# Spreading the reciprocal row sums of attention by two DMAs instead of by TensorE and ScalarE

## What is computed

```python
q, k, v = x @ Wq + bq, x @ Wk + bk, x @ Wv + bv      # (2048, 512), 8 heads of width 64
scores  = einsum('bdsh,bdth->bdst', q, k) / sqrt(8)
weights = softmax(scores, axis=-1)                    # over the 2048 keys
feats   = einsum('bdst,bdth->bdsh', weights, v)
out     = feats @ Wo + bo
x       = layernorm(x + out)
```

## Time and profile before

| | us |
|---|---|
| median of 3 runs | 1293.24 (1292.84 to 1294.88) |
| span of the profiled execution, first to last instruction | 1289.5 |
| the profiled execution's own time | not among the times shown; the median stands 3.7 above the span |
| attention, first spreading to last | 161 to 936 |
| PE busy (share of span) | 1255.7 (97%) |
| DVE busy | 998.2 (77%) |
| ACT busy | 919.8 (71%) |
| POOL busy | 513.2 (40%) |

### The profile page before, as it was taken

One profiled execution on the slowest core, in us unless ns is written; L12 is line 12 of the kernel. 1 busy time (PEld: TensorE's weight loads), 2 busy tenths in 40 slices (PEclk: granted clock), 3 DMA queues, 4 the chain that ended last, 5 costly groups with the idle time before them and its releaser, 6 DMA issues. The chain is left out here.

```text
span 1289.5 us, 24161 instructions
## 1 busy us (share of the span) xinstructions
PE 1255.7 (97%) x8128; PEld 1058.8 (82%) x8128; DVE 998.2 (77%) x1891; ACT 919.8 (71%) x1643; POOL 513.2 (40%) x508
## 2 busy tenths in 40 slices
PE   7999999999999999999999999999988999999896
PEld 5888799889889889989989989989866877777642
DVE  5623688789889979979979979979866777776387
ACT  5421589778878868868868868878833877778343
POOL 0002223234524524524533533542543666676412
PEclk9999999999999999999999999999999999999999
DMA  8788466212424424323423423543578999997698
GB/s 282 258 283 289 155 196 223 69 42 84 147 66 138 145 70 139 125 88 110 146 84 101 155 89 88 156 136 120 178 272 326 386 386 385 346 339 252 237 426 335
DMA packets 90951, 253.14 MB, mean 196 GB/s; under 512 B 16824, under 2 KB 39480, under 8 KB 87504
## 3 DMA queue, kind: packets, MB, share of 16 engines
q1 hardware_dynamic: 70608, 196.78, 44.9%
q0 software_dynamic: 17920, 50.62, 10.2%
q10 hardware_dynamic: 2304, 4.20, 0.8%
HBM read 177.87 MB, written 134.91 MB: 243 GB/s over the span
## 5 line engine op out<-in xcount | busy, mean ns | idle before, releaser
L967 ACT ACTIVATE p_hi<-slot 128x512 fp32r<-128x512 f32 x512 | 278.5, 596 | 108.9 <-PE slot L1594 105.5
L807 POOL TENSOR_TENSOR p_lo<-prob,p_hi 128x512 fp32r<-128x512 f32 x128 | 166.1, 1297 | 441.9 <-ACT prob L969 441.7
L1607 PE MATMUL slot<-k_stack,q_stack 128*128 128x512 f32 x1024 | 300.1, 415 | 0.0
L984 ACT ACTIVATE prob<-prob,row_min 128x1024 f32<-128x1024 f32 x256 | 296.8, 1160 | 0.1
L1307 DVE TENSOR_TENSOR p_lo<-slot,p_hi 128x512 fp32r<-128x512 f32 x384 | 250.8, 681 | 52.5 <-ACT p_hi L967 51.1
L1594 PE MATMUL slot<-ident,prob 128*128 128x128 f32 x2048 | 265.8, 273 | 1.3 <-ACT prob L984 1.3
L1632 PE MATMUL pv_acc<-p_hi,v_pair 128*128 128x256 f32 x1024 | 263.1, 290 | 2.6 <-POOL p_lo L807 1.8
L1632 PE MATMUL pv_acc<-p_lo,v_pair 128*128 128x256 f32 x1024 | 253.7, 281 | 0.0
L1594 PEld LDWEIGHTS slot<-ident,prob 128*128 128x128 f32 x2048 | 229.5, 141 | 1.9 <-issue 1.7
L1632 PEld LDWEIGHTS pv_acc<-p_hi,v_pair 128*128 128x128 f32 x1024 | 192.6, 188 | 16.1 <-issue 5.7
L1632 PEld LDWEIGHTS pv_acc<-p_lo,v_pair 128*128 128x128 f32 x1024 | 192.8, 188 | 12.9 <-issue 3.3
(11 more groups left out here) (196 smaller groups left out, 1974.4 us busy)
## 6 DMA issues: line engine op xcount, KB each, us to landing
disp_hbm<-zero_hbm SPq DMA_DIRECT2D x64, 518.0 KB, 6.3
rows_all<-disp_hbm SPq DMA_DIRECT2D x64, 518.0 KB, 12.8
y_hbm<-zero_hbm SPq DMA_DIRECT2D x48, 512.0 KB, 4.4
got<-y_hbm SPq DMA_DIRECT2D x15, 1536.0 KB, 19.0
q_stack<-q_hbm SPq DMA_DIRECT2D x128, 128.0 KB, 3.1
up_pair<-in_L_ffn_w_up SPq DMA_DIRECT2D x26, 512.0 KB, 9.5
down_w<-in_L_ffn_w_down SPq DMA_DIRECT2D x32, 256.0 KB, 12.0
q_hbm<-q_hi SPq DMA_DIRECT2D x8, 512.0 KB, 2.7
```

Source lines behind the costliest of these rows:

```text
L807: e.tensor_tensor(p_lo[1][:, 2:4, :], prob[:, m % 2, :, (4 * u + 2) * P:(4 * u + 4) * P], p_hi[1][:, 2:4, :].bitcast(F32), ALU.subtract).t ...
L967: e.activation(p_hi[b][:, two, :], view[:, two, :], ACT.Copy).then_inc(a_phi, 1)
L984: e.activation(keys, keys, ACT.Exp, bias=row_min[:, me % 2, j, 1:2], scale=-1.0, accum_out=row_sum[:, me % 2, j, half:half + 1]).then_inc( ...
L1607: made = e.matmul(slot[:, n * BANK:(n + 1) * BANK], qs[:, part, j * P:(j + 1) * P], k_stack[:, ms % H, keys], start=part == 0, stop=part == 1)
```

## The change

The reciprocals go by HBM: at u = 1 SP stores `row_inv` (128 partitions of 2 values, 1 KB in all) to one of two places in HBM, and at u = 3 it loads that 1 KB into each of the 128 partitions of `scaled`. PE's two transposes and ACT's copy go. In HBM the order is partition, then query tile, so `scaled`, and with it `moved` and `feats`, holds the queries interleaved (query p of tile j at place 2 p + j); the multiply reads `pv_acc` with the matching pattern, and the output projection takes each tile's queries with a step of 2. The zero fillings are put elsewhere in SP's queue.

```diff
+        inv_hbm = hbm("inv_hbm", (2, P, QT))
...
+        d_inv, d_spread = sem("dma_inverse_store"), sem("dma_inverse_spread")
...
+        def by_query(t):
+            return t[:, :].rearrange("d (p j) -> d p j", j=QT)
+        def of_tile(t, j):
+            return t.rearrange("d (p j) -> d p j", j=QT)[:, :, j]
... SP
+            def store_inverse(m):
+                e.wait_ge(v_inv, m + 1)
+                if m >= 2:
+                    e.wait_ge(d_spread, 16 * (m - 1))
+                e.dma_start(inv_hbm[m % 2], row_inv[:, :]).then_inc(d_inv, 16)
+            def spread_inverse(m):
+                e.wait_ge(d_inv, 16 * (m + 1))
+                if m:
+                    head_out(e, m - 1)
+                else:
+                    e.wait_ge(v_vlo, NS)
+                    e.wait_ge(g_vlo, NS)
+                    e.wait_ge(a_vhi, 2 * NS)
+                e.dma_start(scaled[:, :], inv_hbm[m % 2].rearrange("p j -> (p j)").partition_broadcast(P)).then_inc(
+                    d_spread, 16)
             jobs = []
             for s in range(LAST + LAG + 2):
+                m, u = divmod(s - LAG, STEPS)
+                if 0 <= m < NCH * H and u == 1:
+                    store_inverse(m)
+                elif 0 <= m < NCH * H and u == 3:
+                    spread_inverse(m)
                 if s < LAST and s % STEPS == STEPS - 1 and s // STEPS + 2 < NCH * H:
                     load_q(s // STEPS + 2)
...
-                elif 2 * STEPS <= s < 2 * STEPS + E - Z_EARLY:
-                    zero_disp(range(Z_EARLY + s - 2 * STEPS, Z_EARLY + s - 2 * STEPS + 1))
-                elif s % 4 == 0 and E <= s < E + 4 * NZ:
-                    e.dma_start(y_pieces[(s - E) // 4], zero_hbm[:, 0:2 * C]).then_inc(d_yzero, 16)
+                elif s >= 2 * STEPS and s % STEPS < 2:
+                    first = Z_EARLY + 3 * (s // STEPS - 2) + 2 * (s % STEPS)
+                    zero_disp(range(first, min(first + 2 - s % STEPS, E)))
+                if s % STEPS == 1 and E <= s < E + STEPS * NZ:
+                    e.dma_start(y_pieces[(s - E) // STEPS], zero_hbm[:, 0:2 * C]).then_inc(d_yzero, 16)
... ACT
-                if 0 <= r < LAST and u == 3:
-                    e.wait_ge(p_spread, m + 1)
-                    if m:
-                        head_out(e, m - 1)
-                    e.activation(scaled[:, :], misc[:, 0:QC], ACT.Copy).then_inc(a_spread, 1)
... DVE
-                    e.wait_ge(a_spread, mv + 1)
+                    e.wait_ge(d_spread, 16 * (mv + 1))
                     e.wait_ge(p_pv, 4 * mv + 4)
-                    if mv:
-                        head_out(e, mv - 1)
-                    e.tensor_tensor(scaled[:, :], pv_acc[:, 0:QC], scaled[:, :], ALU.mult).then_inc(v_scaled, 1)
+                    e.tensor_tensor(by_query(scaled), pv_acc[:, 0:QC].rearrange("d (j p) -> d p j", j=QT),
+                                    by_query(scaled), ALU.mult).then_inc(v_scaled, 1)
...
                     e.wait_ge(a_exp, 4 * m + 4)
+                    if m:
+                        e.wait_ge(d_inv, 16 * m)
                     e.tensor_tensor(row_inv[:, :], row_sum[:, m % 2, :, 0], row_sum[:, m % 2, :, 1],
                                     ALU.add).then_inc(v_sum, 1)
... PE
-                    made = e.matmul(bank_of(c, j)[:, :], feats[:, k, j * P:(j + 1) * P], wo_sb[:, k, :],
+                    made = e.matmul(bank_of(c, j)[:, :], of_tile(feats[:, k, :], j), wo_sb[:, k, :],
                                     start=k == 0, stop=k == KC - 1)
...
-                if 0 <= r < LAST and u == 3:
-                    e.wait_ge(v_inv, m + 1)
-                    wait_misc()
-                    for j in range(QT):
-                        made = e.transpose(misc[:, j * P:(j + 1) * P], row_inv[:, j:j + 1].to_broadcast([P, P]),
-                                           ident[:, :])
-                    made.then_inc(p_spread, 1)
-                    misc_read.append((a_spread, m + 1))
```

More of the change, by code:

```diff
@@ L216, in build @@
         p_k, p_q, p_v = (sem(f"pe_{n}") for n in ("k", "q", "v"))
-        p_scores, p_turned, p_pv, p_spread = (sem(f"pe_{n}") for n in ("scores", "turned", "pv", "spread"))
+        p_scores, p_turned, p_pv = (sem(f"pe_{n}") for n in ("scores", "turned", "pv"))
         p_proj, p_x1t, p_gate, p_rank = (sem(f"pe_{n}") for n in ("proj", "x1_turned", "gate", "rank"))
@@ L220, in build @@
         a_xhi, a_whi, a_khi, a_qhi, a_vhi = (sem(f"act_{n}") for n in ("x_hi", "w_hi", "k_hi", "q_hi", "v_hi"))
-        a_exp, a_phi, a_copy, a_spread = (sem(f"act_{n}") for n in ("exp", "p_hi", "p_copy", "spread"))
+        a_exp, a_phi, a_copy = (sem(f"act_{n}") for n in ("exp", "p_hi", "p_copy"))
         a_x1t, a_score = sem("act_x1_turned"), sem("act_score")
```

## The result

The changed kernel takes 1441.78 us (median of 4 runs, 1435.4 to 1443.68) against 1293.04 us before (1292.28 to 1294.88) in the same comparison: the ratio is 1.1142, 95% interval 1.1117 to 1.1167. The forecast was 1301 with a range of 1279 to 1318. The direction was the likeliest one, the size was missed by 141 us. The profiled execution took 1441.1 us with a span of 1439.2 us; the kernel before had a span of 1289.5.

A forecast was written before the change was run, and what follows sets the result against it. PE was taken to bound attention, busy 100 of 100 us. PE's gain of -12.3, zeros +15.3, head 60 +3.0 and even heads +2.0 gave +8.0 us on 1293.24, so 1301 us, range 1279 to 1318.

The forecast's parts named there:

- the new chain: SP's store, q loads, feats in even heads, then spread; the store was taken at 2.0 us, bounds 1.9 and 2.9.
- the room of odd heads: Odd heads' spread was to land in time by 2.5 us, even with the slow store.
- T + 4.9: Forecast landing of odd heads' spread without other traffic, 4.9 us after the end of the reciprocal.
- The spread: Load of 128 rows of 1 KB from HBM, priced like a q_stack load at 2.9 us, bounds 1.9 and 3.9.
- T + 7.4: Forecast landing of even heads' spread, which waits for feats, 7.4 us after the end of the reciprocal.
- T + 7.45: Latest landing of the spread before PE is held up, 7.45 us after the end of the reciprocal.
- rival D: Store and spread over 1 us slower in every head; odd heads hide it, even don't; 1.5 us more near 1345; chance 0.12.
- the 2.0 for even heads: Cost to PE of spreads landing slightly late in some 24 even heads, 0 to 10 us, taken as 2.
- Zeros ahead of the spread: Heads 0 to 7: two zero pieces queued between store and spread delay the landing, costing 15.3 us.
- the loop of reciprocal, spread and multiply: Pace of heads 0 to 7, with DVE's work to the next reciprocal at 4.15 us: five loops of 13.05, three of 13.55.
- the pace by PE: In attention PE is busy 100 of 100 us and sets the pace, a step taking 2.75 us.
- the 0.22 us a head: PE time held up by the removed transposes at each head's end, 14.1 us over 64 heads.

The follow-up runs named there:

- e7: Changed kernel, the 8-byte pieces gathered into one SBUF partition and the spread reading it 128 times, no HBM; 1.1283 of the kernel before.
- e4: Changed kernel, the store writing the same kilobyte as two rows of 512 bytes from a constant tile; 1.0339 of the kernel before.
- e6: Changed kernel with the store of two 512-byte pieces, the spread reading 128 different HBM rows of zeros; 1.0120 of the kernel before.
- e1: Changed kernel, all three zero pieces of a head issued behind its spread; 1.0919 of the kernel before.
- e13: e11 with the output projection and what follows it one step later in the orders of PE, DVE and POOL; 1.0085 of the kernel before.
- e14: e11 with the output projection and what follows it two steps later in the orders of PE, DVE and POOL; 1.0011 of the kernel before.
- e11: e12 with the q loads ahead of the store and the zeros behind the spread; 1.0148 of the kernel before.
- e12: Changed kernel, DVE copying pv_acc unscaled, POOL multiplying a step later, spread to 64 partitions not waiting for feats; 1.0283 of the kernel before.
- e5: Kernel before with the change's interleaved layout, stepped reads and zero order, spreading still on PE and ACT; 1.0000 of the kernel before.
- e2: Changed kernel, the two q_stack loads issued ahead of the store of the reciprocals; 1.0624 of the kernel before.
- e8: e7 with q loads first, zeros behind the spread, and the spread waiting only for the join of the head before; 1.0741 of the kernel before.

## Why the prediction was wrong, step by step

**The step that failed** is the first price of the new chain: "The store holds 1 KB in 128 pieces of 8 bytes; no row shows such a write", bounded by 1.9 and 2.9, and "I take 2.0, since the moved row has the same kind of issue and little data." It took from 2.6 to 5.4 us, median 4.0 in odd heads from 8 on, and it also slowed what was in the queue with it: q_stack from 3.1 to 3.5, feats from 2.0 to 3.6. The row that I priced it by, moved, has 64 pieces of 1 KB and goes to SBUF; e7 shows that 128 pieces of 8 bytes to SBUF take 1.9 us indeed. The other, zero_hbm, has pieces of 296 bytes. A row that I did not look at, x_hbm, has the right goal and count, 128 pieces to HBM, and with 2 KB in each it takes 2.0. And e4 shows what a store of two pieces of 512 costs, no more than no store at all. So what fails is small pieces and HBM together; neither alone is slow. Worth some 104 us of the 149 (e4), with what it does to its neighbours. The Trainium skill, "DMA: Bandwidth & Descriptors", specifications, says that transfers under 512 bytes are done by read-modify-write. By that rule the wide store is cheap and the change's is dear, and the two runs agree; that it is this mechanism no run shows. The prediction named it against the store and set it aside for the room of odd heads, 2.5 us; store and spread together used up more. In odd heads the landing moved from T + 4.9 to T + 8.7: 2.0 of the 3.8 are the store, the other 1.9 the spread.

**The spread, "2.9 us. That all rows read the same kilobyte may make it a little faster or slower; bounds 1.9 and 3.9."** It took 2.9 to 8.6 over all, medians 4.8 in odd and 3.8 in even heads. The same kilobyte is worth some 28 us of time (e6). What is in the queue with the spread does the rest, as far as the landings show it: the median is 6.7 in heads 0 to 7, behind zeros. By the fit of the Trainium skill, "DMA: Bandwidth & Descriptors", anatomy of one DMA, 2.0 us plus bytes over 436 GB/s, I estimate 2.3; the page takes that fit for DMAs issued from GpSimd, these are SP's, and no spread in the trace was so short.

**Even and odd heads.** The forecast had odd heads safe at T + 4.9 and even ones just in time at T + 7.4. They landed at T + 8.7 and T + 9.3 (medians), both over T + 7.45. That was rival D, to which I gave 0.12: its mechanism is what was measured, its size not. D let odd heads hide everything, and priced 1.5 us more at 48 for the even heads and 12 for the first eight. Its own sum is off as well: on the forecast's 1301 these give 1361, or 1353 with the even heads among the first eight counted once and the 2.0 for even heads taken off, not 1345. The excess over T + 4.9 was 3.8 us in odd heads, so they lost 42.2 us too, and the even ones with heads 8k lost 71.8.

**Zeros ahead of the spread**: forecast +15.3, measured 19 by e1, and 30.2 with the slow store in the same loop. The loop of reciprocal, spread and multiply was right: DVE's part behind the multiply, put at 4.15, was 3.70 in nearly all of these heads.

**The missed path** is feats and the output projection. The forecast asked of feats only when it frees the way for the spread, not who else waits for it. In the kernel after feats is issued at T + 1.7 (median, at most 2.9) behind the store and the q loads and lands at about T + 5.7 in even heads, T + 6.2 in heads 8k; it used to land at T + 2.1 and 2.6. PE's projection then stood 3.5 us at head 32, and heads 8k cost 4.8 us more each (medians 15.34 and 20.14), up to 7.8 more in head 48; the seven lost 28.5 us. e13 and e14 show the cause, in the kernel with time to land: put the projection later, and the loss is gone.

**The clock**, left out of the forecast. Behind some of these stops PE runs slower for a while. After the wait of 3.30 us at 507.36 (the row of the timeline), one group of eight turns takes 1.91 us where 1.04 is its length, and the granted clock of the 3.5 us is 0.52, against 1.00 in the 6 us before it:

```profile
507.36 0.39 PE L1661 MATMUL pv_acc<-p_hi,v_pair 128*128 128x256 f32 x1 [3.30 <-DVE scaled L1341]
...
509.01 1.91 PE L1623 MATMUL slot<-ident,prob 128*128 128x128 f32 x8
```

```profile
496.00:502.00 6.00, 6.00 (x47) 5.65 (x45) 5.66 (x12) 5.63 (x10) 4.91 (x6) 1.00 0.76 171
507.50:511.00 3.50, 3.50 (x17) 3.50 (x18) 3.47 (x9) 1.89 (x4) 0.72 (x1) 0.52 0.38 144
```

0.52 is near the lower level, 1.2 GHz. So this stop cost PE its length and about 1.7 us more (half of the 3.5 us), and that part hides in busy time. The clock records of the trace have 21 such stretches in attention, 78.5 us in all, at half of full speed; half of that, 39 us, is what they cost, and PE's busy time there is 39 us longer, although it has 128 transposes less. Not every stop has one: they stand at stops of 2.2 to 4.8 us, and stops of up to 2.6 us at other places have none. The kernel before and e14 have no such stretch in attention, e4 has three.

**Right** were: the pace by PE and the 0.22 us a head (e11 and e12, 11.01 for 11.23); the deadline near T + 7.45, as far as the traces bound it (in the kernel after a spread that landed at T + 7.04 cost its head nothing, and all later than T + 8.6 cost 0.7 us or more outside the heads behind 8k; between these some paid and some did not); the multiply at 424 ns with its step, the weight loads at no cost (e5; line 1550's 220 ns in the kernel after are 196 outside the slow stretches of the clock and 327 in them); the new order of the zeros costs nothing where there is no spread to hold up (e5).

**Open**: what happens between the last packet of an 8-byte store and its semaphore; from which piece size on it is slow, as only 8, 512 and 2048 bytes were seen; why the reading of one kilobyte is slow from HBM and slower still from one partition; and how much of the 12 us that should have been gained in e14 is lost to POOL. A second pv_acc, which would give the spread a whole head to land, was not tried.

## What to carry to other kernels

Price a DMA that no row shows by a row with the same goal and the same piece size, not the same kilobytes: 128 pieces of 8 bytes cost 1.9 us into SBUF and 2.6 to 5.4 into HBM, where 128 pieces of 2 KB cost 2.0, and they slowed their neighbours. Where no row has both, take the gap as the largest unknown, and try it alone first. Where two dependent DMAs take the place of a few hundred ns on an engine, count the time from their trigger to their deadline, put both ends of every unknown in that sum together, and follow also what they push back in the same queue (here feats, and with it the projection). A stop of PE can cost more than its length: look at the granted clock behind it, as a list of waits does not show that part.

## What the runs showed of the hardware

- Stores of 128 pieces of 8 bytes to HBM: 2.6 to 5.4 us, median 3.7 (4.0 in odd heads, and 3.0 there with the q loads issued ahead of it instead of behind, e2). Their packets are over after 1.0 us. Two pieces of 512 bytes: 1.1 (e4). 128 pieces of 2 KB: 2.0 (kernel before). The 8-byte pieces to SBUF: 1.9 (e7).
- One kilobyte spread to 128 partitions: from HBM 2.9 to 8.6 us in the kernel after, median 4.4, the longest behind zeros; from one partition of SBUF median 6.4 in e7 and e8, the shortest 6.3. Loads of 128 different rows of the same size, as of q_stack in e4 and e6: 3.0.
- PE's granted clock fell to its lower level, 1.2 GHz, 21 times in the attention of the kernel after, at stops of 2.2 to 4.8 us. Eight matmuls of 512 columns that took 3.60 us took 5.1 to 6.7 there.
